# Query blocks ahead of a softmax division, one exponential taken apart, and value copies issued earlier in a fused attention and expert kernel

## What is computed

```python
def attention_block(x):                       # x: 16 x 512 x 256, already normalised
    h = layernorm(x, g1, b1)
    q, k, v = split_heads(h @ qkv_w + qkv_b)  # 16 heads of 16
    s = einsum(q, windows_of_15(k)) / 4       # each token sees 7 to the left and right
    h = einsum(softmax(s), windows_of_15(v)) @ proj_w + proj_b
    x = x + h
    return x + gelu(layernorm(x, g2, b2) @ fc1_w + fc1_b) @ fc2_w + fc2_b

def experts(x):
    main = gelu(x @ W1m + b1m) @ W2m + b2m
    top2 = top_k(softmax(mean(x, tokens) @ w_gate + b_gate), 2)
    e = sum over top2 of weight * (gelu(x @ W1e[e] + b1e[e]) @ W2e[e] + b2e[e])
    return a * main + (1 - a) * e

x = x + attention_block(layernorm(x))
x = x + experts(layernorm(x))
```

## Time and profile before

| what | value |
| --- | --- |
| three runs, us | 1984.82, 1988.66, 1984.09; median 1984.82 |
| the profiled execution | 1985.26 us, its span 1983.5 us |
| mean granted TensorE clock | 0.996 of full speed |
| PE busy | 1922.4 us, 97% of the span |
| DVE busy | 1364.2 us, 69% |
| ACT busy | 1151.5 us, 58% |
| POOL busy | 855.2 us, 43% |
| DMA | 122.40 MB, mean 62 GB/s |
| turns | turn 0 takes some 107 us, turns 1 to 15 some 120 us each, turn 16 the rest |

### The profile page before, as it was taken

How to read it: one execution, slowest core, us unless ns; L and a number is a source line. 1 busy time by engine, 2 the same in 40 slices (tenths; PEclk the granted TensorE clock), 3 DMA queues, 4 the chain that set the end, 5 groups by cost and what they waited for, 6 DMA issues and landing times.

```text
span 1983.5 us, 57523 instructions
## 1 busy us (share of the span) xinstructions
PE 1922.4 (97%) x23694; PEld 1728.9 (87%) x23694; DVE 1364.2 (69%) x2271; ACT 1151.5 (58%) x1833; POOL 855.2 (43%) x781
## 2 busy tenths in 40 slices
PE   6899999999999999999999999999999999999999
PEld 5789889898898988889898898988989889898998
DVE  6576776867767576676867768677585766768643
ACT  4565556655656565565555556556565655655554
POOL 4436234262433625245262443624336252452625
PEclk8999999999999999999999999999999999999999
DMA  4131220313103131131311203122031311313121
GB/s 124 50 81 55 56 64 28 92 55 74 58 27 91 44 92 44 44 76 38 92 55 48 72 28 92 55 67 63 28 92 44 91 45 40 80 38 92 44 60 54
DMA packets 237053, 122.40 MB, mean 62 GB/s; under 512 B 113564, under 2 KB 235768, under 8 KB 236792
## 3 DMA queue, kind: packets, MB, share of 16 engines
q1 hardware_dynamic: 234708, 117.57, 22.2%
q10 hardware_dynamic: 2084, 1.16, 0.2%
HBM read 85.52 MB, written 8.39 MB: 47 GB/s over the span
## 4 chain that ended last, share of the span: by engine, by line
PE 76%; DVE 10%; ACT 8%; issue 4%; POOL 1%; SPq 1%; DMA 0%; ACTq 0%; POOLq 0%; DVEq 0%
PE psB L233 42%; PE psA L233 24%; DVE hr_lo L533 3%; PE psA L1063 3%; PE psA L1100 2%; PE psA L976 2%; ACT hr_hi L824 2%; PE psA L1075 2%; ACT pr L873 2%; DVE pr L616 1%; DVE qm L576 1%; DVE smax L612 1%; ACT L820 1%; ACT L873 1%; ACT hf L820 1%
## 5 line engine op out<-in xcount | busy, mean ns | idle before, releaser
L533 DVE TENSOR_TENSOR hr_lo<-hf,hr_hi 128x512 fp32r<-128x512 f32 x512 | 477.2, 932 | 494.7 <-ACT hr_hi L824 493.9
L824 ACT ACTIVATE hr_hi<-hf 128x512 fp32r<-128x512 f32 x512 | 324.0, 633 | 282.2 <-PE psB L233 194.3
L439 POOL TENSOR_SCALAR wx_hi<-raw 128x512 fp32r<-128x512 f32 x256 | 184.6, 721 | 632.1 <-PE psB L233 360.7
L441 POOL TENSOR_TENSOR wx_lo<-raw,wx_hi 128x512 fp32r<-128x512 f32 x256 | 415.2, 1622 | 21.4
L820 ACT ACTIVATE hf<-psB,b1x 128x512 f32<-128x512 f32 x256 | 175.2, 684 | 198.7 <-PE psB L233 197.8
L233 PE MATMUL psB<-wx_hi,hr_hi 128*128 128x256 f32 x1024 | 287.4, 281 | 0.2
L233 PE MATMUL psB<-wx_hi,hr_lo 128*128 128x256 f32 x1024 | 286.3, 280 | 0.0
L233 PE MATMUL psB<-wx_lo,hr_hi 128*128 128x256 f32 x1024 | 285.7, 279 | 0.0
L233 PE MATMUL psB<-z_hi,wx_hi 128*128 128x512 f32 x512 | 211.9, 414 | 0.0
L233 PE MATMUL psB<-z_hi,wx_lo 128*128 128x512 f32 x512 | 202.4, 395 | 0.0
L233 PEld LDWEIGHTS psB<-wx_lo,hr_hi 128*128 128x128 f32 x1024 | 192.4, 188 | 10.2
(11 more groups left out here) (151 smaller groups left out, 4710.0 us busy)
## 6 DMA issues: line engine op xcount, KB each, us to landing
raw<-in_L_ffn_W1e SPq DMA_DIRECT2D x256, 128.0 KB, 2.3
raw<-in_L_ffn_W2e SPq DMA_DIRECT2D x256, 128.0 KB, 2.2
vb<-vs SPq DMA_DIRECT2D x64, 192.0 KB
vb<-vs SPq DMA_DIRECT2D x62, 160.0 KB
out_x<-acc SPq DMA_DIRECT2D x32, 256.0 KB, 2.2
xin<-in_L_attn_x SPq DMA_DIRECT2D x15, 512.0 KB, 3.7
tm<-in_L_ffn_b2e SPq DMA_DIRECT2D x32, 128.0 KB, 3.0
raw<-in_L_attn_fc_w SPq DMA_DIRECT2D x8, 256.0 KB, 4.4
```

The costliest lines, as they stand in the source:

```text
L439: g.tensor_scalar(wx[0][:, s, :], raw[:, s, :], 1.0, 0.0, ALU.mult, ALU.add).then_inc(w_hi.sem, 1)
L441: g.tensor_tensor(wx[1][:, s, :], raw[:, s, :], wx[0][:, s, :].bitcast(f32), ALU.subtract).then_inc(w_lo.sem, 1)
L533: v.tensor_tensor(hr[1][:, c % 2, :], hf[:, c % 3, :], hr[0][:, c % 2, :].bitcast(f32), ALU.subtract).then_inc(h_lo.sem, 1)
L824: a.activation(hr[0][:, c % 2, :], hf[:, c % 3, :], ACT.Copy).then_inc(h_hi.sem, 1)
```

## The change

The edits are on DVE, ACT and SP. PE and POOL keep their order, and the arithmetic is the same.

- DVE, turns 1 to 15: `query_blocks(t, 2)` goes from step 4 (after `h_low` of chunk 4) to step 3 (after `h_low` of chunk 3), and `normalise(t, 1)` from step 3 to step 4.
- ACT, all turns: `exp(t, 2)` goes from step 8 to step 7. In turns 1 to 15 the Gelu of chunk 8 then stands between the two exponentials. DVE: `normalise(t, 2)` goes from step 9, behind `gather` of chunk 7 and ahead of `h_low` of chunk 9, to step 8 behind `h_low` of chunk 8. `normalise(t, 3)` stays in step 10, but now ahead of `h_low` of chunk 10 instead of behind it.
- SP, turns 1 to 15: the 12 DMAs of `windows` are issued after expert chunk 0's load instead of after expert chunk 3's.

```diff
@@ sync
-                            elif n == RING and t < ROWS:
+                            elif n == 1 and t < ROWS:
                                 windows(sp, t, range(6))
@@ vector
                         if q == 3:
                             normalise(t, 0)
-                        elif q == 9:
-                            normalise(t, 2)
+                        elif q == 10:
+                            normalise(t, 3)
...
                     elif q == 3 and t < ROWS:
+                        query_blocks(t, 2)
                         if t == 0:
-                            query_blocks(t, 2)
+                            normalise(t, 1)
+                    elif q == 4 and t > 0 and t < ROWS:
                         normalise(t, 1)
-                    elif q == 4 and t > 0 and t < ROWS:
-                        query_blocks(t, 2)
...
+                    elif q == 8 and t < ROWS:
+                        normalise(t, 2)
                     elif q == 9 and t < ROWS:
                         attended_low(t, 0)
-                    elif q == 10 and t < ROWS:
-                        normalise(t, 3)
@@ scalar
+                    elif q == 7:
+                        exp(t, 2)
                     elif q == 8:
-                        exp(t, 2)
                         exp(t, 3)
                         attended_high(t, 0)
```

## The result

The changed kernel takes 1965.11 us (median of 4 runs, 1963.99 to 1967.88) against 1985.51 us for the kernel before in the same comparison (4 runs, 1984.09 to 1988.66). The ratio is 0.9897, 95% interval 0.988 to 0.9914. The gain is 20.4 us where 30 were forecast: the direction and the range hold, and a third of the gain did not come. The time lies above the 1950 to 1962 of the forecast itself, in the band that was given to rival A. The profiled execution took 1966.04 us, its span 1964.3 us.

A forecast was written before the change was run, and what follows sets the result against it. PE was taken as the bound, busy 97%, with 33.0 us of idle time to be won; 3.0 us stay at the last turn, so 1985.26 - 30 = 1955.3, said as 1955 us. Forecast 1950 to 1962, range 1950 to 1968.

The forecast's parts named there:

- rival A: At unit 3's turn: ACT's own work holds the chain, so PE waits there; 1976 us; chance with its half 0.13.
- What bounds the kernel: PE, busy 97% of the span: only its idle time at scores and turns can be won, 33.0 us.
- Part 1: DVE, steps 3 and 4: query blocks before second division end the scores' wait; PE 1.60 us earlier, no price.
- Part 2: SP: value copies start 3.67 us earlier, in time for the first attend; alone worth nothing, keeps the query blocks' gain.
- Part 3: ACT, steps 7 to 9: exponential 2 alone adds two 1.28 us table loads, paid by idle stretches.
- rival C: ACT: each of two added table loads costs 1.28 us more in its new place; 1993 us, slower; chance 0.02.
- Part 4: DVE, steps 8 and 10: earlier divisions end unit 2's 0.35 us wait; about 0.2 us stays at unit 3's turn.
- Rival B: DVE, steps 7 and 8: moved POOL splits delay exponential 3's input, up to 5.4 us; 1999 us, slower; chance 0.03.

The follow-up runs named there:

- e3: Kernel before with only the query blocks put ahead of the second division on DVE: 1968.68 us, ratio 0.9924.
- e2: Changed kernel with the value copies issued behind expert chunk 3 again, POOL's splits back in their old place: 1962.75 us, ratio 0.9888.
- e4: Kernel before with query blocks ahead of the second division and value copies issued behind expert chunk 0: 1968.51 us, ratio 0.9911.
- e5: Changed kernel with POOL's bias moved from step 7 to step 11: 1957.42 us, ratio 0.9866.
- e6: Changed kernel with unit 2's division behind the gather again and POOL's bias in step 11: 1955.65 us, ratio 0.9859.
- e1: Changed kernel with unit 2's division back in step 9, behind the gather: 1963.76 us, ratio 0.9897.
- e7: Kernel before with only exponential 2 in step 7 and the earlier divisions of units 2 and 3: 1981.23 us, ratio 0.9982 (10 runs).
- e8: Changed kernel with unit 2's division behind the gather again and exponential 2 back in step 8: 1967.4 us, ratio 0.9909.
- e9: Changed kernel with gather ahead of unit 2's division, POOL's bias in step 11 and exponential 2 back in step 8: 1956.29 us, ratio 0.9853.
- e11: Changed kernel with gather ahead of unit 2's division, bias in step 11 and value copies issued behind expert chunk 1: 1957.7 us, ratio 0.9859.

## Why the prediction was right, and where its size was off

**What bounds the kernel** held. PE's work did not change (1920.3 us against 1922.4), and what it stood idle at the three places was what could be won.

**Part 1** held where it was priced. In the changed kernel the scores of unit 2 start at 729.40, 0.21 us behind the start of the last product. e3 shows it by itself: the wait for `qm` goes from 19.2 us to nothing, and the waits ahead of the turns stay.

**Part 2** was right in what it said of the copies and wrong in its price. Left in place they would have cost something (5.4 and 5.7 us in e2 and e3), within the bounds of 0 to 1.6 us a turn; moved, they cost nothing. The failed step is "Alone this edit is worth nothing; it keeps part 1's gain", with the contention put off to a rival of 0.03. e3 against e4 shows the edit keeping nothing: the splits, sent into DVE's steps 5 to 7 where the bias already was, cost as much as the copies had. This is the term that was mis-sized: nothing in the sum, 15.1 us of PE's time in the changed kernel.

**Part 3** held to 0.02 us in turn 6, where DVE's `shift` comes in time; in eight other turns ACT waited for it. From chunk 7's rounded copy to chunk 9's Gelu were 10.01 us before (743.35 to 753.36) and are 10.03 after, with two table loads more. ACT in turn 6:

```profile
738.69 0.63 ACT L824 ACTIVATE hr_hi<-hf 128x512 fp32r<-128x512 f32 x1 [0.77 <-PE psB L233]
739.34 1.28 ACT L873 ACT_TABLE_LOAD   x1
740.64 0.85 ACT L873 ACTIVATE pr<-pr 128x768 f32<-128x768 f32 x1
741.50 1.28 ACT L820 ACT_TABLE_LOAD   x1
742.80 0.69 ACT L820 ACTIVATE hf<-psB,b1x 128x512 f32<-128x512 f32 x1
...
747.42 1.28 ACT L820 ACT_TABLE_LOAD   x1
748.72 0.69 ACT L820 ACTIVATE hf<-psB,b1x 128x512 f32<-128x512 f32 x1
```

Each switch stands in the trace with 0.02 us beside its load, so rival C and the Trainium skill's drain of 1380 ns ("ScalarE: Activation LUTs", "What ACT_TABLE_LOAD costs") are not found here: the whole switch is 1.30 us.

**Part 4** had an omission, which decides where the lateness shows. It moved unit 2's division ahead of the gather and asked only who reads the division. It did not ask who waits for the instruction it was put in front of: PE's `chunk_down` of chunk 8, for the two banks. On paper there was room. At the predicted times unit 2's division would have ended at 751.7 and the two halves of the gather at 752.4 and 753.1. PE began this `chunk_down` at 752.85 in the timeline of before, and it reaches the second half six products, 0.7 us, later. DVE's lengthening ate its own idle time first and then these 0.45 us. The omission by itself cost nothing that can be seen: e5, which keeps the order, is within 0.4 us of e6 over the 15 turns, and e1, which undoes it under the same POOL work, gains 1.4 us by the medians. The price of unit 3's step was mis-sized too: e5 and e7 show 6.1 us of waiting there instead of 3.0, since the split of expert chunk 5 lengthens the division.

**Rival B** was the right mechanism with too small a chance, and its price came mostly from another reader. It foresaw up to 5.4 us of lengthening and a limit of 4.5, at the input of exponential 3. The lengthening measured is 4.5 us in the four operations shown. In turn 6 `shift` ends at 744.40 + 0.96 = 745.36, just as exponential 3 is due (ACT's table load began at 744.17), and what is late is the gather, two steps on. In eight turns exponential 3 is late as well, by up to 0.8 us: the very sign that the prediction named for B. In the changed kernel no further wait of PE comes of it. Where the gather stands ahead of the division it does: e1, e4 and e8 have ten waits of 1.75 us at unit 3's turn, and each is in a turn in which ACT waited for line 607; in e5, e6 and e9 to e11, with the bias later, there is neither from turn 1 on. The lateness passed the slack by about a microsecond and not by the 2.9 of B's worst case, so 15.1 us of the 33 were lost and the kernel was not slower.

**The range held partly by luck.** 1965 us lies outside 1950 to 1962 and in what was set aside for rival A, but A did not happen: nothing waits at unit 3's turn, and e3 shows none of the gain kept there. The range reached to 1968 for A's sake; B, whose mechanism gave the result, had been priced as a slowdown, 1999 us.

**The sum by terms.** Forecast 30 us. In the 15 turns the changed kernel is 22.1 us shorter (1803.7 to 1781.6), of which the gather's wait has taken 15.1 that were not in the sum, and 3.0 us of waiting forecast at unit 3's turn did not occur, since the gather's wait comes ahead of it. 33.0 - 15.1 = 17.9 are thus explained. The other 4.2 were in no term: turn 2 of the kernel before holds a stretch at the lower clock (below), some 1.7 us, and its list of waits has 2.8 us for "issue" in turns 1 to 16 that the changed kernel's hasn't. What these are is not shown.

```profile
PE psA L1100 <- issue: 1.7, 3, 0.8
...
PE psA L1075 <- issue: 0.6, 1, 0.6
PE psB L233 <- issue: 0.5, 1, 0.5
```

e5 and e6 win 29.7 and 30.1 us in the same 15 turns. They are free of the low clock too and have 1.3 us of "issue", so some 27 of the 30 are what the edits give when POOL's bias is out of the way. The last part of the difference lies in turn 0, whose order did not change: it took 107.2 us before and 110.1 us after. The windows from 30 to 55 us, before and then after, show the granted clock (third number from the end) at 0.73 and 0.66, which is 1.7 us of the 2.9 (an estimate, 25 x 0.07); the rest is open. Over all thirteen profiled executions turn 0 takes from 107.2 to 110.2 us, with no regard to the edits. 22.1 - 2.9 = 19.2 us is what lies between the two profiled executions, 1985.26 and 1966.04.

```profile
30.00:55.00 25.00, 15.56 (x519) 13.15 (x517) 13.75 (x18) 12.76 (x24) 9.80 (x6) 0.73 0.47 119
```

```profile
30.00:55.00 25.00, 14.26 (x408) 12.00 (x408) 12.84 (x17) 12.12 (x23) 8.83 (x5) 0.66 0.49 118
```

## What to carry to other kernels

A DMA that is issued earlier pushes back those behind it, and the engine that consumes them moves with them: ask beside which work of which other engine it then runs, and add what already runs there. When an instruction is moved ahead of another on a strictly ordered engine, list the readers of the one it overtakes, the buffers that it frees among them, and not those of the moved one alone: that is where lateness will show. Read a sign in all turns and not in one: in turn 6 ACT waits for nobody at exponential 3, in eight others it does. Where two engines lengthen each other's operations, moving one operation of the idle engine (the bias here, 6 to 8 us of 1965) is cheaper than reordering the busy one.

## What the runs showed of the hardware

**A POOL operation and a DVE operation hold each other up, nearly for the whole operation.** In the changed kernel POOL's bias took 3.39 us where it took 2.41, and the DVE operation beside it 2.90 us where it takes 0.68 alone. POOL's ended 2.27 us after DVE's line 700 beside it did (739.63), and DVE's line 533 ended at 742.45, 0.55 us after POOL's at 741.90; both are nearly their time without the other. The 1.78 us row that the prediction called too short for a full lock-out fits as well: POOL's operation had begun 0.65 us before it, at 729.77, and DVE ended at 732.20, 0.55 us after POOL's 731.65. The DVE addition of line 700 had a median of 1.22 us with POOL idle (e2) and 2.19 us beside a split (changed kernel). This agrees with the exclusive lock of the Trainium skill ("SBUF — State Buffer", "Who interferes with whom"). What I had not expected is how it adds up: four operations in a row lost 4.5 us beside 7.1 us of POOL's.

**The clock can fall right behind a wait of PE of under 2 us.** In turn 2 of the kernel before the granted clock is 0.50 from 252.2 to 255.6 us, the lower of its two levels, 1.2 GHz, and 2.4 GHz ahead of it and behind. That turn took 122.0 us against 119.7 and 120.5 for its neighbours. PE's timeline shows what came before, the wait for the query blocks; the busy times of the stretch follow:

```profile
250.58 0.62 PE L1063 MATMUL psA<-kT,qm 64*64 64x48 f32 x28 [1.52 <-DVE qm L576]
```

```profile
252.20:255.60 3.40, 3.40 (x13) 2.98 (x12) 1.80 (x4) 3.37 (x7) 0.00 (x0) 0.50 0.62 175
```

The thirteen profiled executions hold five such stretches between turn 1 and turn 15, each 3.4 us long, which at half the clock is some 1.7 us lost: this one, two in e1 (277.1 and 993.9), one in e4 (518.2) and one in e7 (972.1). Each begins 1.0 to 1.6 us after PE has stood idle for 1.25 to 1.77 us. Most waits of that length are not followed by one: in the kernel before one of twelve is. The executions of e2, e6 and e9 to e11, which have no wait of PE over 1.1 us there, have no such stretch; nor have the changed kernel, e3, e5 and e8, which have one to four such waits each. So a long wait can cost more than its own length, and part of what removing one gives may be this. Why it falls behind one wait and not behind another these runs do not show.
